# A decoder layer on one Trainium2 core: the attention stage's PSUM rings and the order of its matmul groups are changed

## The reference, cut to what matters

```python
q = _split_heads(hidden_states @ Wq + bq)        # x is (4, 512, 512), 16 heads of 32
k = _split_heads(hidden_states @ Wk + bk)
v = _split_heads(hidden_states @ Wv + bv)
ctx = _local_attention(q, k, v)                  # softmax over a window around each block of 128
idx = _global_index(q)                           # bos, the 62 queries of largest norm, eos
qg = jnp.take_along_axis(q, idx[..., None], axis=-2)
g_scores = jnp.einsum('nhqd,nhkd->nhqk', qg, k) / math.sqrt(d)
g_ctx = jnp.einsum('nhqk,nhkd->nhqd', jax.nn.softmax(g_scores, axis=-1), v)
```

## Time and profile before

| | us |
|---|---|
| median of 3 runs | 1066.62 (1061.22 to 1067.45) |
| the profiled execution | 1064.37, of which its span is 1062.7 |
| PE / DVE / ACT / POOL busy in the span | 945.0 / 765.9 / 601.7 / 529.3 |
| attention, from its first turn on PE to the last line 764 | 187.6 to 470.2 |

### The profile page before, as it was taken

The page is one execution under the profiler, slowest core; times in us unless marked ns, Lnnn a source line. Parts: engine busy times, 40 slices in busy tenths (PEclk is TensorE's granted clock), DMA queues, the critical chain, the costliest instruction groups (busy, mean ns, idle before and its releaser), DMA issues. The chain is left out here.

```text
span 1062.7 us, 18006 instructions
## 1 busy us (share of the span) xinstructions
PE 945.0 (89%) x5112; PEld 713.1 (67%) x5112; DVE 765.9 (72%) x1347; ACT 601.7 (57%) x913; POOL 529.3 (50%) x442
## 2 busy tenths in 40 slices
PE   5899998799999999965999999992888999999981
PEld 4677786444444444424888889991877888888970
DVE  4425554777777787638888888854776999999974
ACT  3443211577676767744344344441766888888863
POOL 3450000265555556527565566623344777777734
PEclk9999999799999999986999999996888999999995
DMA  8466400543342526202112111122689544444467
GB/s 258 159 225 220 189 1 6 137 97 99 80 111 67 118 61 142 98 27 75 50 61 61 60 59 53 46 68 85 196 239 274 92 73 75 72 76 79 79 161 225
DMA packets 80883, 115.72 MB, mean 109 GB/s; under 512 B 15680, under 2 KB 37056, under 8 KB 80832
## 3 DMA queue, kind: packets, MB, share of 16 engines
q1 hardware_dynamic: 67760, 93.32, 29.3%
q0 software_dynamic: 9760, 20.49, 10.7%
q10 hardware_dynamic: 3312, 1.32, 0.5%
HBM read 74.77 MB, written 40.31 MB: 108 GB/s over the span
## 5 line engine op out<-in xcount | busy, mean ns | idle before, releaser
L1840 DVE TENSOR_TENSOR we_lo<-w_all,we_hi 128x1408 fp32r<-128x1408 f32 (+1 forms) x117 | 191.8, 1668 | 13.6 <-ACT we_hi L1772 11.9
L867 DVE TENSOR_REDUCE maxima<-ps_s 128x8 f32<-128x512 f32 x240 | 150.8, 685 | 51.2 <-PE ps_s L723 50.4
L1772 ACT ACTIVATE we_hi<-w_all 128x1408 fp32r (+1 forms) x117 | 165.7, 1419 | 37.7 <-PE e_ps_y L1913 19.2
L676 POOL TENSOR_TENSOR pair_sum<-probs 128x2048 f32<-128x2048 f32 x30 | 137.3, 4577 | 92.3 <-ACT probs L839 92.3
L839 ACT ACTIVATE probs<-ps_st 128x512 f32<-128x512 f32 x256 | 143.1, 598 | 69.5 <-PE ps_st L778 66.1
L1744 POOL DMA_INDIRECT x_dram<-e_y,who x39 | 104.5, 2679 | 106.6 <-ACT e_y L1789 76.8
L1510 PE MATMUL ps_gu<-sw_hi,x2T_hi 128*128 128x352 f32 (+1 forms) x256 | 88.1, 344 | 1.9 <-issue 1.7
L1738 POOL DMA_INDIRECT xg<-x_dram,who x39 | 79.8, 2047 | 14.3 <-issue 11.1
L1510 PE MATMUL ps_gu<-sw_lo,x2T_hi 128*128 128x352 f32 (+1 forms) x256 | 83.9, 328 | 0.0
L1510 PE MATMUL ps_gu<-sw_hi,x2T_lo 128*128 128x352 f32 (+1 forms) x256 | 83.6, 327 | 0.0
L778 PE MATMUL ps_st<-q_more,k_more 128*128 128x512 f32 x160 | 72.8, 456 | 4.4 <-ACT probs L839 3.0
(11 more groups left out here) (266 smaller groups left out, 2479.2 us busy)
## 6 DMA issues: line engine op xcount, KB each, us to landing
qk_dram<-qk_ctx SPq DMA_DIRECT2D x32, 512.0 KB, 3.0
q_more<-qk_dram SPq DMA_DIRECT2D x60, 128.0 KB, 3.0
k_more<-qk_dram SPq DMA_DIRECT2D x60, 128.0 KB, 3.1
w_all<-in_L_ffn_w_gate_dram SPq DMA_DIRECT2D x8, 704.0 KB
w_all<-in_L_ffn_w_up_dram SPq DMA_DIRECT2D x8, 704.0 KB
q_first<-qk_dram SPq DMA_DIRECT2D x36, 128.0 KB, 3.1
k_first<-qk_dram SPq DMA_DIRECT2D x36, 128.0 KB, 3.3
x_tile<-in_x_dram SPq DMA_DIRECT2D x16, 256.0 KB, 2.7
```

What stands on the lines that cost most here:

```text
L676: pool.tensor_tensor(pair_sum[:, h], probs[:, 2 * h], probs[:, 2 * h + 1], ALU.add).then_inc(added, 1)
L867: dve.tensor_reduce(by_tile[:, t, j, 1:9], bank(p, x).rearrange("p (g n) -> p g n", n=S // 8), axis=AX.X, op=ALU.max).then_inc(s_reduced, 1)
L1772: act.activation(w_hi[kind][:], raw(base, kind), ACT.Copy).then_inc(s[kinds[kind] + "_hi"], 1)
L1840: dve.tensor_tensor(w_lo[kind][:], raw(base, kind), w_hi[kind][:].bitcast(F32), ALU.subtract).then_inc(s[kinds[kind] + "_lo"], 1)
```

## The change

* `ps_st` gets a third bank, in place of the bank that turned shift rows and turned row sums shared. `turn` now writes into the ring of `ps_st` as a 17th entry of each unit, and `back` writes its row sums into the ring of `ps_s` as a 17th entry (`RING` = 17). ST(s) waits for the exp three before it; ST(2) waits for all four shift copies. S(7) waits for the reciprocal of the row sums, and `back` for the first three maxima of unit u+2.
* GpSimd copies the bar of a unit into a fixed tile `bar_u`; VectorE reads that in place of a slice of `c.bar`.
* The groups on TensorE move: `weigh(u-1, 3)` and `sums(u-1, 0)` at step 5, `sums(u-1, 1)` and `weigh(u, 0)` at 11, and `turn(u+1)`, `back(u-1)`, `weigh(u, 1)`, `weigh(u, 2)` at 15. `take_out` and `take_sum` follow exp 5 and exp 11, the four `take_shift` all follow exp 15.
* VectorE's `normalise(u-1)` moves behind the maxima x = 0 to 4 of unit u+2; in the last unit `last_pairs(1)` stands behind it.

```diff
+RING = NU + 1
...
+        bar_u = m.sb("bar_u", [P, TT, HPG])
         ps_s = m.ps("ps_s", [P, BANKS, S])
-        ps_st = m.ps("ps_st", [P, 2, S])
+        ps_st = m.ps("ps_st", [P, BANKS, S])
...
-        ps_both = m.ps("ps_turn_rows", [P, S])
-        ps_turn = ps_both[:, 0:S // 2].bitcast(BF16)
-        ps_rows = ps_both[:, S // 2:S // 2 + TT * HPG].rearrange("p (t j) -> p t j", j=HPG)
...
         def bank(p, x):
-            return ps_s[:, (NU * p + x) % BANKS, :]
+            at = x - EARLY if x >= EARLY else x - EARLY - 1
+            return ps_s[:, (RING * (p - 1) + at) % BANKS, :]
+        def rows_bank(p):
+            return ps_s[:, (RING * p + NU) % BANKS, 0:TT * HPG].rearrange("p (t j) -> p t j", j=HPG)
+        def st_bank(p, s):
+            return ps_st[:, (RING * p + s) % BANKS, :]
+        def turn_bank(p):
+            return st_bank(p, NU)[:, 0:S // 2].bitcast(BF16)
...
+                pool.tensor_copy(bar_u[:], c.bar[:, :, 0:HPG]).then_inc(bar_taken, 1)
...
                     pool.tensor_copy(vu[:].rearrange("p t d -> p (t d)"), slot(c.v, u)).then_inc(v_in, 1)
                     if is_last(u):
                         return
+                    pool.wait_ge(turn_ready, u + 1)
+                    pool.tensor_copy(bar_u[:], c.bar[:, :, bass.ds(HPG * (u + 1), HPG)]).then_inc(bar_taken, 1)
...
-                    need(pe, s_reduced, NU * u + x - BANKS + 1)
+                    if EARLY <= x < EARLY + 2:
+                        need(pe, s_reduced, NU * u + x - 1)
+                    elif x == EARLY + 2:
+                        need(pe, recip_done, u - 2)
+                    else:
+                        need(pe, s_reduced, NU * u + x - BANKS + 1)
...
-                def turn(u):
+                def turn(u, before):
                     pe.wait_ge(turn_ready, u + 1)
-                    need(pe, shift_ready, HPG * u)
-                    need(pe, recip_done, u - 1)
+                    need(pe, exp_done, NU * u - 2)
...
-                def back(u):
+                def back(u, after, scores):
                     pe.wait_ge(o_taken, u + 1)
                     pe.wait_ge(sum_taken, u + 1)
                     pe.wait_ge(normed, u + 1)
+                    pe.wait_ge(s_reduced, scores)
...
-                            pe.wait_ge(shift_ready, HPG * u + j + 1)
-                        need(pe, exp_done, NU * u + s - 1)
+                            pe.wait_ge(shift_ready, HPG * u + (HPG if s == 2 else j + 1))
+                        if s < 2:
+                            need(pe, exp_done, NU * u + s - 1)
+                        elif s > 2:
+                            need(pe, exp_done, NU * u + s - BANKS + 1)
...
-                        if not first:
-                            if s == 7:
-                                weigh(u - 1, 3)
+                        if s == 5 and not first:
+                            weigh(u - 1, 3)
+                            sums(u - 1, 0)
+                        if s == 11:
+                            if not first:
                                 sums(u - 1, 1)
-                            if s == 10:
-                                back(u - 1)
-                        if s == 12:
                             weigh(u, 0)
+                        if s == 15:
+                            if not last:
+                                turn(u + 1, p)
+                            if not first:
+                                back(u - 1, p, NU * U if isinstance(u, int) and u > U - 3 else NU * (u + 2) + 3)
                             weigh(u, 1)
-                        if s == 13 and not last:
-                            turn(u + 1)
-                        if s == 15:
                             weigh(u, 2)
-                            sums(u, 0)
                     if last:
+                        sums(u, 0)
                         weigh(u, 3)
                         sums(u, 1)
...
-                        if s == 7 and not first:
+                        if s == 5 and not first:
                             take_out(u - 1)
-                        if s == 8 and not first:
+                        if s == 11 and not first:
                             take_sum(u - 1)
-                        if s >= 14 and not last:
-                            for j in range(2):
-                                take_shift(u + 1, (p + 1) % SLOTS, 2 * (s - 14) + j)
+                    if not last:
+                        for j in range(HPG):
+                            take_shift(u + 1, (p + 1) % SLOTS, j, p)
...
-                    if not first:
-                        normalise(u - 1)
-                    if last:
-                        last_pairs(1)
                     if not (isinstance(u, int) and u > U - 3):
                         for x in range(EARLY):
                             reduce(u + 2, (p + 2) % SLOTS, x)
+                    if not first:
+                        normalise(u - 1, p)
                     if last:
-                        normalise(u)
+                        last_pairs(1)
+                        normalise(u, (p + 1) % SLOTS)
```

More of the change, by code:

```diff
@@ L721, in score @@
                         pe.wait_ge(unit_in[p], NDMA * uses + (NDMA if p else 0))
-                    need(pe, s_reduced, NU * u + x - BANKS + 1)
+                    if EARLY <= x < EARLY + 2:
[4 more added lines that the diff above has]
+                        need(pe, s_reduced, NU * u + x - BANKS + 1)
                     pe.matmul(bank(p, x), q4[p][0:BR, j, t * P:(t + 1) * P], k4[p][0:BR, j, :],
                               start=True, stop=True).then_inc(s_done, 1)
-                def turn(u):
+                def turn(u, before):
                     pe.wait_ge(turn_ready, u + 1)
-                    need(pe, shift_ready, HPG * u)
-                    need(pe, recip_done, u - 1)
+                    need(pe, exp_done, NU * u - 2)
                     for t in range(TT):
-                        last = pe.transpose(ps_turn[:, t * P:(t + 1) * P], turn_in[:, t * P:(t + 1) * P], c.ident_bf[:])
+                        last = pe.transpose(turn_bank(before)[:, t * P:(t + 1) * P], turn_in[:, t * P:(t + 1) * P], c.ident_bf[:])
                     last.then_inc(turned, 1)
@@ L761, in back @@
                     pe.wait_ge(normed, u + 1)
+                    pe.wait_ge(s_reduced, scores)
                     for t in range(TT):
-                        pe.matmul(ps_rows[:, t, :], sumT[:, t * P:(t + 1) * P], first_rows[:], start=True, stop=True)
+                        pe.matmul(rows_bank(after)[:, t, :], sumT[:, t * P:(t + 1) * P], first_rows[:], start=True, stop=True)
                         last = pe.transpose(ps_back[:, t * P:(t + 1) * P], outT[:, t * P:(t + 1) * P], c.ident[:])
@@ L814, in _, with take_shift @@
             def _(act):
-                def take_shift(u, p, j):
+                def take_shift(u, p, j, before):
                     if j == 0:
@@ L818, in take_shift @@
                         need(act, st_done, NU * (u - SLOTS + 1))
-                    act.activation(q4[p][BR:P, j, :], ps_turn[HD * j:HD * (j + 1), :], ACT.Copy).then_inc(shift_ready, 1)
+                    act.activation(q4[p][BR:P, j, :], turn_bank(before)[HD * j:HD * (j + 1), :], ACT.Copy).then_inc(shift_ready, 1)
                 def take_out(u):
@@ L851, in _ @@
                 for j in range(HPG):
-                    take_shift(0, 0, j)
+                    take_shift(0, 0, j, SLOTS - 1)
                 units(act, unit)
@@ L877, in step @@
                         dve.wait_ge(row_step, 6 * u + k[0])
-                    bar = c.bar[:, :, bass.ds(HPG * u, HPG)]
                     dve.wait_ge(s_reduced, NU * u + NU)
+                    dve.wait_ge(bar_taken, u + 1)
                     dve.tensor_reduce(m_win[:].rearrange("p t j -> p t j"), windows, axis=AX.X, op=ALU.max)
                     step(dve.tensor_reduce(m_all[:], by_tile, axis=AX.X, op=ALU.max))
-                    step(dve.tensor_tensor(m_bar[:], m_all[:], bar, ALU.add))
+                    step(dve.tensor_tensor(m_bar[:], m_all[:], bar_u[:], ALU.add))
                     step(dve.tensor_tensor(m_row[:], m_bar[:], m_win[:], ALU.max))
@@ L889, in row_maxima, with normalise @@
                     k[0] += 1
-                    step(dve.tensor_copy(bar_rows, bar))
+                    step(dve.tensor_copy(bar_rows, bar_u[:]))
                     dve.sem_inc(turn_ready, 1)
-                def normalise(u):
+                def normalise(u, after):
                     dve.wait_ge(backed, u + 2)
-                    dve.reciprocal(rsum[:], ps_rows).then_inc(recip_done, 1)
+                    dve.reciprocal(rsum[:], rows_bank(after)).then_inc(recip_done, 1)
                     dve.wait_ge(recip_done, u + 1)
```

9 lines of the change are left out of this document (5 added, 4 removed).

## The result

The median rose from 1064.78 to 1103.42 us (four runs of each kernel, 1061.22 to 1067.45 and 1094.88 to 1104.96). The ratio is 1.0369, with a 95% interval of 1.0336 to 1.0402: slower by 3.7%, outside the range given. The profiled execution took 1104.96 us, its span 1103.2.

What follows compares the result with a forecast made beforehand. The bound was a loop in which GpSimd's long sum holds VectorE's `m_bar`, delaying S(3). 1064.4 + 0.7 + 0.1 - 0.3 - 2.1 + 1.4 = 1064.2, plus 2.2 for the median: 1066 us, range 1056 to 1081.

Steps and rivals of the forecast that it cites:

- The clock: TensorE's idle of 1.8 us before S(3) may lower the granted clock; most likely one unit hit, +1.4 us.
- Rival B: The clock falls in most units, adding 11 to 28 us, total about 1083; chance 0.13.
- Items 1 to 5: Like unit's chain from ST(0): shift rows ready at 12.13 us against 12.35, then 5.04 to its end against 4.77.
- item 6: Sum for a like unit: 17.17 us against 17.12, +0.05; for thirteen of them +0.7.
- A: No measurable difference, 1066 us, bounds 1059 to 1074, each like unit within 0.3 either way; chance 0.72.
- Item 3: On GpSimd, the bar copy takes 0.2 us and costs nothing; the sum over chunks 0 and 1 starts at 6.75.
- Item 4: In VectorE's `row_maxima`, GpSimd's sum holds `m_bar` until 11.36 because it has two inputs; the fixed bar copy changes nothing.
- Rival C: GpSimd doesn't hold `m_bar`; units 1.7 us shorter, total 1043; chance 0.05.
- Item 7: The ends of the run: unit 0 +0.1 us, unit 14 about -0.3, the last unit -2.1.
- Item 8: What costs nothing, such as VectorE's division moved behind the maxima, not held by GpSimd's sum over chunks 2 and 3.
- rival E: VectorE's division is held by GpSimd's second sum after all; +16 us, total 1082; chance 0.05.
- Rival D: The third bank and early TensorE group gain more; 1% needs the stretch before exp 7 ending 0.8 earlier; chance 0.05.

Runs made afterwards that it cites:

- `FILL` = 3: The changed kernel with S(2) moved from step 13 to 14, ahead of S(3)'s wait, and issued three times; 1074.26 us, ratio 1.0095 to the kernel before.
- `FILL` = 1: The changed kernel with S(2) moved from step 13 to 14, ahead of S(3)'s wait, and issued once; 1100.67 us, ratio 1.0336 to the kernel before.
- the one-input version: The changed kernel with `row_maxima` rewritten so that no instruction has two inputs in SBUF; 1100.67 us, ratio 1.0331 to the kernel before.
- the old order: The kernel before with one added VectorE reduction of 1.74 us over constants ahead of a unit's first maxima; 1102.89 us, ratio 1.0366 to the kernel before.
- FILL = 7: The changed kernel with S(2) moved from step 13 to 14, ahead of S(3)'s wait, and issued seven times; 1069.66 us, ratio 1.0054 to the kernel before.

## Why the prediction was wrong

**The step that failed is "The clock".** It took one unit hit at 1.4 us. Measured in the profiled execution: twelve of thirteen at 2.96. Both factors were wrong; the first decided, since twelve at 1.4 would have made 17 and one at 2.96 only 3.

*How often.* The prediction had the idle of 1.8 and its place, and set the fall at the earlier trace rows aside because "around that one the matmuls were much sparser". The like units, with their dense matmuls, show that this was no excuse, and the repeated S(2) that the idle is what does it: an idle of 1.29, 0.75 or 0.37 hit three, one and none of thirteen units, 1.69 to 1.75 ten to twelve. (The three with a shorter idle also have more work beside it; idle and work weren't varied apart.) A second argument was right in kind and misled: that a longer unit shifts the stretch against whatever decides, so that one unit is hit and the next not. `FILL` = 3 shows just that, with every fourth unit hit. But a unit hit as here lasts 20.48 to 20.62, and after it the next fall comes at nearly the same place again. The clock right after it fell in unit 1, and in unit 12 (columns as above):

```profile
224.23:224.63 0.40, 0.40 (x3) 0.21 (x1) 0.40 (x2) 0.00 (x0) 0.00 (x0) 0.51 0.00 0
449.50:449.63 0.13, 0.00 (x1) 0.00 (x1) 0.13 (x2) 0.00 (x0) 0.00 (x0) 0.55 0.00 0
```

That is 13.6 after ST(0) in unit 1, where S(3) has started at 13.2, and 13.05 in unit 12, just before S(3). Unit by unit the fall comes a little earlier (0.14 at the most), until a unit is spared: 13 here, 8 with `FILL` = 1, 11 in the one-input version. So in these three the hits come in rows of twelve, seven and ten units. What it is that the shift runs against stays open.

*How much.* 1.4 reckoned the fall for part of the tail. It covers nearly all: S(3), ST(15), S(4), `turn`, `back` and both `weigh`, 7.33 at 0.54 for the 4.39 at 1.00 of unit 8 with `FILL` = 1, which is 2.94. But 1.4 wasn't out of reach: hits cost 1.6 where the stretch stands at 0.72 (`FILL` = 3, and one unit of `FILL` = 1), and 1.3 in the old order. Why the clock stayed low longer in the changed kernel's units isn't shown; that more stands behind the wait only set how much there was to lose.

**Rival B** was the mechanism, at 0.13 and 1083. Its price was bounded by 14 x 2.0 = 28; 12 x 2.96 = 35.5 lies beyond it. The page of the Trainium skill that was weighed with the clock ("TensorE: Matmul & The Clock Gate", section "A second HAM failure mode: psum-queue depth-cycling") spoke for B, and the trace of after agrees in kind: by it each unit could be hit, and twelve were.

**Items 1 to 5 held in the main.** The chain to R came out at 12.20 against 12.13. After R: S(3) +0.97 against +0.87, and from S(3) to the next ST(0) 4.39 at full clock against 4.17, most of it between `back` and the first `weigh` (1.31 in unit 13 against 1.11). So an undisturbed looped unit is 17.56 where item 6 said 17.17. That is 0.39, more than the 0.3 that A allowed, and some 5 us in all. The kernel without falls, FILL = 7, has units of 17.57 and 1069.66: A's range held it, with some luck, since the last unit gained 0.9 more than forecast and the 1.4 for the clock stood in the sum.

**Item 3**, the bar copy: 0.20 as taken, hidden. **Item 4**: `m_bar` ends 0.03 after GpSimd, with 1.95 in its row (about 2.1 said), and the fixed copy changes nothing; shown by the versions with and without it. Its reason, "that it has two", is only part of the rule. Rival C fell with this. **Item 7**: the last unit gained 3.0, not 2.1; unit 14 0.2, not 0.3. **Item 8**: the division, 0.69 beside a GpSimd sum that runs from 349.22, isn't held, so rival E fell. Rival D: R moved by 0.15 only, as said.

## What to carry to other kernels

Price an idle of TensorE by what stands behind it as well as by its length: where it grows beyond what the trace has at full clock, reckon that the clock can fall in most passes, and for all the work that follows, and put independent matmuls there or shorten the wait. Follow a wait to its root before moving work: a small VectorE instruction that ends as a long GpSimd one does was cured here by the order of the two, not by what it reads. A wait put on GpSimd is only free if its result is wanted late, so look up who takes it next.

## What the runs showed of the hardware

A standstill of 1.75 us in units of 17.6, in the same place of each, was enough to keep TensorE at 1.2 GHz for a third of the time (7.33 of 20.50 at 0.54; 0.83 over 227 us), though single units with the same standstill were spared, and seven repeated matmuls in that place, three with some effect already, were enough to end it. The loss can be larger than the idle itself: 2.96 of clock for 1.75 of standing in the changed kernel, 1.6 for 1.29 with `FILL` = 3.

Beside a GpSimd `tensor_tensor` of 4.6 us a VectorE `tensor_tensor` of 16 columns took 1.95 instead of 0.175 and a `tensor_scalar` 1.55 instead of 0.20, each until GpSimd's end, while reductions of the same size (0.19) went through.
